# Second attention: signs of the fifth count used as a mask, copies and keeps regrouped, failing rows mended after the first keeps

## The chip, the cores and the metric

The kernel runs on one NeuronCore of a Trainium2 chip. The metric is the device time of one execution, in microseconds (us); less is better. The engines named below are TensorE (PE in the profile), VectorE (DVE), ScalarE (ACT), GpSimd (POOL) and SyncE (SP), each with its own queue of instructions. They meet only at semaphores. "Us" always means microseconds of the profiled execution unless a sentence says that it means the median of the runs.

## The reference, cut to what matters

A two-layer language-model tower on token ids of shape 2 x 1024, width 1024, 32 heads, 8 key/value heads, head width 32. The first layer is token mixing, causal attention and a top-2 mixture of experts; the second is an attention that keeps only 128 keys for each query, and a second mixture. The change lies in the second attention:

```python
qr = apply_rope(q, cos, sin)
kr = apply_rope(k, cos, sin)
draft = jnp.einsum('bhqd,bhkd->bhqk', qr, kr)
causal_future = qi[:, None] < ki[None, :]
draft = draft + jnp.where(causal_future, neg, jnp.asarray(0.0, dtype))
num_remain = max(min(Sq, MIN_REMAIN), Sq - int(Sq * MASK_OUT))      # 128
_, draft_indices = jax.lax.top_k(draft, num_remain)
mask = jnp.full((B, H, Sq, Sq), neg, dtype)
mask = mask.at[b_idx, h_idx, s_idx, draft_indices].set(0.0)
mask = jnp.where(causal_future[None, None, :, :], neg, mask)
scores = jnp.einsum('bhqd,bhkd->bhqk', qr, kr) / np.sqrt(HD).astype(np.float32) + mask
attn = jax.nn.softmax(scores, axis=-1)
out = jnp.einsum('bhqk,bhkd->bhqd', attn, v)
```

So each of the 2 x 32 x 1024 rows of scores needs its 128th largest value among its allowed keys; everything under it gets weight zero.

## The kernel before, in words

The program runs stage after stage: token mixing, projection, first attention, mixture, projection, second attention (`kept_attention`), mixture. All that changes is in `kept_attention` and in the constants that it reads.

**Tiles.** Heads go in pairs; there are 32 pairs. A pair has 16 tiles: for each of its two heads `m`, eight strips `i` of 128 queries, each (i+1)*128 keys wide (`TILES`). Strips with i = 0 have at most 128 keys and need no selection; the other 14 are `RANKED`, widths 256, 384, ... 1024 for each head. `x` holds the scores of a pair, `prob` their exponentials, both with two buffers.

**Slots.** The stage is a software pipeline in slots. In slot s four pairs are in hand: pair s+1 is scored (TensorE makes `ps_s`, VectorE moves it to `x`, `fetch`), pair s is searched (`count` on ScalarE, `narrow` on VectorE), pair s-1 is ranked and kept (VectorE: `rank_some`, `choose`, `exact_where_needed`, `keep`), and pair s-2 is multiplied with the values (TensorE transposes `prob` into `ps_t`, ScalarE copies it to `probT` in `evac`, TensorE multiplies by `v`, VectorE scales in `normalise`). Two slots make one turn of a hardware loop; four slots stand ahead of it and some behind.

**The search.** Each row has a threshold `t`. `start` sets it from mean and deviation of a sample of the row. Then five times (`PASSES`): ScalarE runs 14 activations Sign(t - x) with a sum (`count`, L1013), so the sum tells how many keys lie above t; VectorE waits for the last of them (`signs_done`) and moves t by a secant step on all 14 tiles at once (`narrow`, L1103 to L1134), where the count is more than 3.6 from the aim of 124.5; ScalarE waits for that (`t_ready`) ahead of its next pass. So a slot has five passes on ScalarE and five steps on VectorE, and each waits for the other.

**Ranking.** In the following slot VectorE makes, for each of the 14 tiles, three instructions (`rank_steps`): a compare with a sum that counts the keys at or over the sixth t and leaves a 0/1 mask `above` (L1145), a multiply-add that pushes those keys to -1e30 in `below` (L1147), and the eight largest of the rest (MAX8, L1150). If the count lies in 121..128, the 128th key is t itself or one of the eight. `choose` picks it for all rows; rows where that fails raise a flag, which is carried across partitions to one register. `exact_where_needed` loads that register and branches: with no failing row it jumps over a long body, else it runs `select_exactly` for the failing tiles, 16 rounds of MAX8 and MATCH_REPLACE over the whole tile.

**What else stands in the parts.** VectorE's work of a slot is written by hand in five parts, one ahead of each `narrow`: `RANKS` says which tiles are ranked in which part (parts 0 to 2), `KEEPS` which tiles are kept and fetched (parts 2 to 4), two keeps and two fetches in turn (`keep_and_fetch`, L1231 and L1241). `normalise` (L1262) stands in part 2, `invert` and `start` in part 4. ScalarE's copies `evac` (L983) are spread over its passes 0 and 1 by the table `after`, its exponentials over the ends of passes 2 and 3 (`EXPS`, L1025). `keep` (L1231) is one instruction a tile: (x >= limit) * prob with its sum.

The order of the work of a part, as the code has it:

```python
RANKS = [[*range(0, TT - 2), TT - 1], [TT - 2, *range(TT + 1, NS)], [TT], (), ()]
KEEPS = [(), (), range(0, 4), range(4, 14), range(14, 2 * TT)]
...
EVAC_PASSES = 2
...
EXPS = {2: range(0, TT + 3), 3: range(TT + 3, 2 * TT)}
```

## Time and profile before

| | us |
|---|---|
| median of 3 runs | 5799.51 |
| the runs | 5797.98 to 5799.66 |
| the profiled execution's own time | 5802.05 |
| its span (first to last instruction) | 5800.2 |
| mean granted TensorE clock over the span | 0.847 of full speed |
| busy: PE / DVE / ACT | 3975.3 / 3821.2 / 3315.8 |

In the page's 40 slices the second attention is the long even stretch from slice 18 to slice 37, where DVE and ACT both stand at 8 tenths and PE at 4 to 5:

```profile
PE   6997888888899989814555545555455554554599
...
DVE  1663666666233346458888888888888888888443
ACT  1113666666100011168888888888888888888200
...
PEclk7998999999999999956777777777777777777799
```

A busy engine is one that executes; where it waits for a semaphore or for its sequencer, it is idle, and the profile names what ended the wait. "issue" means that nothing the profile shows was waited for.

### The profile page before, as it was taken

Reading aid. Unit: us, or ns where it says so; the run is one execution under the profiler, and the core shown is the slowest. Engines: PE = TensorE matmul, PEld = TensorE weight load, DVE = VectorE, ACT = ScalarE, POOL = GpSimd, SP = SyncE. Lnnn points to the kernel's source line nnn. Section 1 sums busy time; section 2 is a strip of 40 time slices with the busy share of each in tenths; the row PEclk is TensorE's granted clock in tenths of the full one; section 3 lists DMA queues with packets and bytes.
Section 4 is the critical chain, followed back from the end, with each engine's and each line's share of the span. In section 5 each row is a group of like instructions: output and inputs, shape, how many; then the busy total and the mean of one; then the engine's idle time right before and its main releaser. Section 6 shows DMA issues by size and latency. Waiting matters only on the chain. (4 is left out here: it accounts for less than half of the span.)

```text
span 5800.2 us, 80523 instructions
## 1 busy us (share of the span) xinstructions
PE 3975.3 (69%) x23480; PEld 2373.9 (41%) x23480; DVE 3821.2 (66%) x10794; ACT 3315.8 (57%) x7698; POOL 289.1 (5%) x213
## 2 busy tenths in 40 slices
PE   6997888888899989814555545555455554554599
PEld 2444555555444444402333323333233332333354
DVE  1663666666233346458888888888888888888443
ACT  1113666666100011168888888888888888888200
POOL 1331000000000023300000000000000000000000
PEclk7998999999999999956777777777777777777799
DMA  3223222212311132310011010110101100010222
GB/s 122 68 68 70 61 56 48 69 47 50 113 44 43 43 101 68 72 30 21 4 24 23 21 23 4 23 23 21 22 5 23 23 21 17 10 23 5 69 66 80
DMA packets 277680, 250.19 MB, mean 43 GB/s; under 512 B 169968, under 2 KB 210048, under 8 KB 277248
## 3 DMA queue, kind: packets, MB, share of 16 engines
q1 hardware_dynamic: 276704, 245.60, 16.2%
q14 instruction: 313, 2.56, 0.2%
q8 instruction: 119, 1.95, 0.1%
q0 software_dynamic: 544, 0.07, 0.0%
HBM read 168.03 MB, written 77.59 MB: 42 GB/s over the span
## 5 line engine op out<-in xcount | busy, mean ns | idle before, releaser
L1013 ACT ACTIVATE a_sign<-a_x,a_state 128x256 fp8e4<-128x256 f32 (+6 forms) x2240 | 1833.7, 820 | 393.6 <-DVE a_state L1134 254.0
L922 PE MATMUL a_ps_s<-a_k,a_q 128*128 128x512 bf16 (+3 forms) x1536 | 479.5, 454 | 749.6 <-DVE a_x L1241 709.4
L950 PE MATMUL a_ps_o<-a_probT,a_v 128*32 128x128 f32 x4608 | 649.2, 289 | 461.8 <-ACT a_probT L983 457.1
L950 PEld LDWEIGHTS a_ps_o<-a_probT,a_v 128*32 128x32 f32 x4608 | 483.6, 115 | 597.3 <-ACT a_probT L983 548.9
L322 PE MATMUL p_ps_qkv<-p_w,p_hT 128*128 128x512 f32 x1536 | 676.6, 597 | 3.3 <-ACT p_hT L360 2.3
L701 ACT ACTIVATE a_prob<-a_ps_s,a_shift 128x640 f32<-128x640 f32 (+7 forms) x512 | 379.9, 742 | 349.0 <-DVE a_shift L743 304.0
L922 PEld LDWEIGHTS a_ps_s<-a_k,a_q 128*128 128x128 bf16 x1536 | 153.8, 123 | 986.6 <-DVE a_x L1241 809.6
L641 PE MATMUL a_ps_t<-a_ident,a_prob 128*128 128x128 f32 x2304 | 369.3, 286 | 164.8 <-ACT a_prob L701 100.9
L743 DVE TENSOR_REDUCE a_shift<-a_ps_s 128x1 f32<-128x640 f32 (+7 forms) x512 | 384.3, 753 | 111.2 <-PE a_ps_s L626 105.2
L322 PEld LDWEIGHTS p_ps_qkv<-p_w,p_hT 128*128 128x128 f32 x1536 | 289.1, 191 | 348.0 <-issue 344.9
L1145 DVE TENSOR_SCALAR_CACHE_REDUCE a_above<-a_x,a_state 128x256 bf16<-128x256 f32 (+3 forms) x448 | 391.8, 875 | 47.3 <-issue 38.2
L1013 ACT ACTIVATION_READ_ACCUMULATOR a_sign<-a_x,a_state 128x1 f32 x2240 | 422.8, 189 | 0.0
L1241 DVE TENSOR_SCALAR_CACHE_REDUCE a_x<-a_ps_s 128x128 f32<-128x128 f32 (+7 forms) x512 | 368.6, 756 | 65.2 <-issue 35.5
L933 PE MATMUL a_ps_t<-a_ident,a_prob 128*128 128x128 f32 x2304 | 409.8, 314 | 0.0
L983 ACT COPY a_probT<-a_ps_t 128x512 f32<-128x512 f32 (+3 forms) x768 | 349.9, 471 | 79.6 <-PE a_ps_t L933 78.9
L1150 DVE MAX8 a_nine<-a_below 128x8 f32<-128x256 f32 (+3 forms) x448 | 371.1, 828 | 33.0
L1231 DVE SCALAR_TENSOR_TENSOR a_prob<-a_x,a_limit,a_prob 128x256 f32<-128x256 f32 (+6 forms) x448 | 380.5, 881 | 10.5 <-issue 3.7
L753 DVE COPY a_probT<-a_ps_t 128x384 f32<-128x384 f32 (+3 forms) x384 | 222.0, 578 | 248.7 <-PE a_ps_t L641 245.2
L1147 DVE SCALAR_TENSOR_TENSOR a_below<-a_above,a_x 128x256 f32<-128x256 bf16 (+3 forms) x448 | 363.3, 811 | 7.2
L641 PEld LDWEIGHTS a_ps_t<-a_ident,a_prob 128*128 128x128 f32 x2304 | 252.3, 142 | 269.1 <-ACT a_prob L701 98.3
L623 PE MATMUL a_ps_s<-a_k,a_q 128*128 128x512 bf16 (+3 forms) x1536 | 339.9, 331 | 23.4 <-DMA a_v<-v 23.4
L1025 ACT ACTIVATE a_prob<-a_x,a_shift 128x256 f32<-128x256 f32 (+6 forms) x448 | 331.2, 813 | 0.0
(200 smaller groups left out, 5292.3 us busy)
## 6 DMA issues: line engine op xcount, KB each, us to landing
a_q<-qk SPq DMA_DIRECT2D x256, 256.0 KB, 4.9
qk<-p_qkT SPq DMA_DIRECT2D x32, 960.0 KB, 6.2
p_h<-h SPq DMA_DIRECT2D x32, 512.0 KB, 7.0
a_k<-qk SPq DMA_DIRECT2D x256, 64.0 KB, 5.1
m_o<-o SPq DMA_DIRECT2D x32, 512.0 KB, 5.4
m_h<-h SPq DMA_DIRECT2D x32, 512.0 KB, 5.5
p_w<-in_wqkv SPq DMA_DIRECT2D x16, 768.0 KB, 12.5
h<-tok_h SPq DMA_DIRECT2D x16, 512.0 KB, 2.6
```

The costliest lines, as they stand in the source:

```text
L322: m = nc.tensor.matmul(ps_qkv[:, n * BANK:(n + 1) * BANK], hT[:, par, k * P:(k + 1) * P], w[:, k, n * BANK:(n + 1) * BANK], start=(k == 0) ...
L641: mm = nc.tensor.transpose(ps_t[:, n % 2, c * P:(c + 1) * P], prob[:, s % 2, (a + c) * P:(a + c + 1) * P], ident[:, :])
L701: nc.scalar.activation(prob[:, s % 2, 0:w], ps_s[:, s % 2, 0:w], ACT.Exp, bias=shift[:, s % 4:s % 4 + 1], accum_out=total[:, u % 2, j:j + ...
L743: nc.vector.tensor_reduce(shift[:, c:c + 1], ps_s[:, s % 2, 0:(i + 1) * P], AX_X, ALU.max, negate=True).then_inc(shift_ready, 1)
L922: nc.tensor.matmul(ps_s[:, n % 2, a:a + w], q[:, y, head, i * P:(i + 1) * P], k[:, y, a:a + w], start=(y == 0), stop=False, skip_group_che ...
L933: mm = nc.tensor.transpose(ps_t[:, (n + 1) % 3, c:c + P], prob[:, par, at:at + P], ident[:, :])
L950: mm = nc.tensor.matmul(ps_o[strip:strip + DH, c:c + P], v[:, b * DH:(b + 1) * DH], probT[:, n % 2, b * P:(b + 1) * P], start=(b == 0), st ...
L1013: ins = nc.scalar.activation(sign[:, off(i):off(i) + w], x[:, par, at:at + w], ACT.Sign, scale=-1.0, saturate=False, bias=state[:, par, 0, ...
L1145: lambda: nc.vector.tensor_scalar(above[:, r, 0:w], x[:, y, at:at + w], tl, None, ALU.is_ge, ALU.add, accum_out=exact[:, n:n + 1]),
L1150: lambda: nc.vector.max(nine[:, n, 1:9], below[:, r, 0:w]),
L1231: nc.vector.scalar_tensor_tensor(out=prob[:, y, at:at + w], in0=x[:, y, at:at + w], scalar=limit[:, r:r + 1], in1=prob[:, y, at:at + w], o ...
L1241: nc.vector.tensor_scalar(x[:, y, at:at + w], ps_s[:, n % 2, 0:w], 1.0, None, ALU.mult, ALU.max, accum_out=top[:, y, n:n + 1]).then_inc(x_ ...
```

## The change

What it does, part by part.

1. **No count on VectorE, and no fifth `narrow`.** ScalarE's fifth pass writes its signs to a buffer of their own, `last` (fp8, all 14 tiles). In the next slot VectorE makes `below` as min(last * 2^116, x): where the sign is -1 (key over t) that is very low, else it is x. The sum of this instruction goes to `over`, and serves only to find keys equal to t. The rank comes from the signs' sum. So ranking is two instructions a tile instead of three, with the threshold of the fourth step instead of the fifth.
2. **The secant.** The brackets begin at a fixed distance of t (`REACH`, `BEND`) instead of at the row's maximum and at mean - 2.5 deviations; misses stand in the bracket instead of sums, ahead of the last step they are multiplied by `FADE`. Two clamps in the first `narrow` and five small copies in `start` go.
3. **Failing rows.** A row fails also if a key equals t. Failing rows get the limit `ALL_KEPT`, so their first `keep` keeps everything; then a code of the failing tiles is loaded to a register; where it isn't zero, `select_exactly` runs for the failing tiles, and tiles kept already are kept once more. The register is loaded, and the branch stands, behind seven keeps instead of ahead of all.
4. **Order.** Ranking stands wholly in parts 0 and 1, seven tiles each. Keeps: 7, 5, 2 tiles in parts 2, 3, 4. Fetches stand behind the keeps of their part in one row: 4, 8, 4 tiles. `normalise` comes behind the fetches of part 2. Exponentials: 6, 5, 5 tiles behind passes 2, 3, 4. The copies `evac` get a pause of 40 in the table between pass 0 and pass 1 and behind pass 1.
5. ScalarE waits for the last transpose of pair s-2 (`turn_done`) ahead of its exponentials, not for `normalise`. One more constant is loaded (`bits`).

```diff
-MASKED = -1e30
+MASKED = -1e18
+REACH, BEND = 600.0, 0.6
+CLOSE = 7.2
+FADE = 0.9
+WIDE = 2.0 ** 116
+ALL_KEPT = -1e17
...
-                    EVAC_PASSES = 2
-                    counted = [sum(2 + i for _, i in (RANKED * EVAC_PASSES)[:k]) for k in range(EVAC_PASSES * NS + 1)]
+                    EVAC_PASSES, BETWEEN = 2, 40
+                    counted = [sum(2 + i for _, i in (RANKED * EVAC_PASSES)[:k]) + BETWEEN * (k // NS)
+                               for k in range(EVAC_PASSES * NS + 1)]
...
-                            ins = nc.scalar.activation(sign[:, off(i):off(i) + w], x[:, par, at:at + w], ACT.Sign, scale=-1.0, saturate=False,
-                                                       bias=state[:, par, 0, n:n + 1], accum_out=state[:, par, 2, n:n + 1])
+                            to = last[:, at:at + w] if p == PASSES - 1 else sign[:, off(i):off(i) + w]
+                            ins = nc.scalar.activation(to, x[:, par, at:at + w], ACT.Sign, scale=-1.0, saturate=False,
+                                                       bias=state[:, par, 0, n:n + 1], accum_out=state[:, par, 3, n:n + 1])
...
-                    EXPS = {2: range(0, TT + 3), 3: range(TT + 3, 2 * TT)}
+                    EXPS = {2: range(0, 6), 3: range(6, 11), 4: range(11, 2 * TT)}
...
-                            lambda: nc.vector.tensor_scalar(above[:, r, 0:w], x[:, y, at:at + w], tl, None, ALU.is_ge,
-                                                            ALU.add, accum_out=exact[:, n:n + 1]),
-                            lambda: nc.vector.scalar_tensor_tensor(out=below[:, r, 0:w], in0=above[:, r, 0:w],
-                                                                   scalar=MASKED, in1=x[:, y, at:at + w], op0=ALU.mult,
-                                                                   op1=ALU.add),
+                            lambda: nc.vector.scalar_tensor_tensor(out=below[:, r, 0:w], in0=last[:, at:at + w],
+                                                                   scalar=WIDE, in1=x[:, y, at:at + w], op0=ALU.mult,
+                                                                   op1=ALU.min, accum_out=over[:, n:n + 1]),
...
                     def exact_where_needed():
 
-                        with dve.If_ne(raised(any_flag), 0):
-
-                            wait_alone(dve, exp_done, (s - 1) * (2 * TT) + 2 * TT, const_in, 64)
+                        dve.reg_load(which, failing[:, :])
+                        with dve.If_ne(which, 0):
+
+                            for k in (64, 32, 16, 8, 4, 2, 1):
+                                nc.vector.tensor_tensor(codes[:, 0:k], codes[:, 0:k], codes[:, k:2 * k], ALU.bitwise_or)
+                                dve.drain()
+                            dve.reg_load(which, codes[:, 0:1])
                             for n in range(NS):
-                                with dve.If_ne(raised(flag[:, n:n + 1]), 0):
+                                dve.reg_alu(this, which, 1 << n, ALU.bitwise_and)
+                                with dve.If_ne(this, 0):
                                     select_exactly(n)
+                                    if n in KEEPS[2]:
+                                        keep(n)
...
-                    RANKS = [[*range(0, TT - 2), TT - 1], [TT - 2, *range(TT + 1, NS)], [TT], (), ()]
-                    KEEPS = [(), (), range(0, 4), range(4, 14), range(14, 2 * TT)]
+                    RANKS = [range(0, TT - 1), range(TT - 1, NS), (), (), ()]
+                    KEEPS = [(), (), range(0, TT - 1), range(TT - 1, NS - 2), range(NS - 2, NS)]
+                    FETCHES = [(), (), range(0, 4), range(4, 12), range(12, 2 * TT)]
 
                     def part(p):
 
                         if st["keep"]:
+                            if p == 0:
+                                wait_alone(dve, signs_done, s * PASSES, const_in, 80)
                             rank_some(RANKS[p])
                             if p == 2:
                                 choose()
+                                dve.wait_ge(exp_done, (s - 1) * (2 * TT) + 2 * TT)
+                            for r in KEEPS[p]:
+                                keep(r).then_inc(prob_ready, 1)
+                            if p == 2:
                                 exact_where_needed()
+                            dve.drain()
+                        if st["score"]:
+                            for n in FETCHES[p]:
+                                fetch(n)
                         if p == 2 and st["value"]:
                             normalise()
-                        keep_and_fetch(KEEPS[p])
...
-                        if st["search"]:
+                        if st["search"] and p < PASSES - 1:
                             narrow(p)
```

In ScalarE's row of a steady slot, the end of pass 0 and the beginning of pass 1. L983 (L988 in the change) is the copy `evac`, L1013 (L1020) the Sign of one tile; the line L215 (L220) is where pass 1 waits for `t_ready`. Before:

```order
L1013 ACTIVATE a_sign,a_state<-a_x,a_state 128x896
L982 REGISTER_ALU
L983 COPY a_probT<-a_ps_t 128x512
L1013 ACTIVATE a_sign,a_state<-a_x,a_state 128x1024
L982 REGISTER_ALU
L983 COPY a_probT<-a_ps_t 128x512
L215 ISA
L1013 ACTIVATE a_sign,a_state<-a_x,a_state 128x256
```

And now:

```order
L1020 ACTIVATE a_sign,a_state<-a_x,a_state 128x1024
L987 REGISTER_ALU
L988 COPY a_probT<-a_ps_t 128x512
L987 REGISTER_ALU
L988 COPY a_probT<-a_ps_t 128x384
L987 REGISTER_ALU
L988 COPY a_probT<-a_ps_t 128x512
L987 REGISTER_ALU
L988 COPY a_probT<-a_ps_t 128x512
L220 ISA
L1020 ACTIVATE a_sign,a_state<-a_x,a_state 128x256
```

One copy stood between the last Sign and the wait; four stand there now, and fewer among the Signs.

In VectorE's row, the end of `choose` and what follows, up to the branch (TENSOR_LOAD is the load of the register, L1218 the `keep`):

```order
L1189 CAST a_codes<-a_codeT 1x32 x4
L1191 TENSOR_REDUCE a_failing<-a_codes 1x1
L1218 SCALAR_TENSOR_TENSOR a_prob,a_total<-a_x,a_limit,a_prob 128x256
L1218 SCALAR_TENSOR_TENSOR a_prob,a_total<-a_x,a_limit,a_prob 128x384
L1218 SCALAR_TENSOR_TENSOR a_prob,a_total<-a_x,a_limit,a_prob 128x512
L1218 SCALAR_TENSOR_TENSOR a_prob,a_total<-a_x,a_limit,a_prob 128x640
L1218 SCALAR_TENSOR_TENSOR a_prob,a_total<-a_x,a_limit,a_prob 128x768
L1218 SCALAR_TENSOR_TENSOR a_prob,a_total<-a_x,a_limit,a_prob 128x896
L1218 SCALAR_TENSOR_TENSOR a_prob,a_total<-a_x,a_limit,a_prob 128x1024
L1250 TENSOR_LOAD a_failing
L1251 COMPARE_AND_BRANCH
```

Seven keeps now stand between the reduction that gives the flag and the load of the flag; before, the load and the branch followed the reduction at once, and no keep stood ahead of them.

## Rows read from the trace of the kernel before

**Rows 1.** The page, busy time (us), share of the span, instructions, of three engines.

```profile
PE 3975.3 (69%) x23480; PEld 2373.9 (41%) x23480; DVE 3821.2 (66%) x10794; ACT 3315.8 (57%) x7698; POOL 289.1 (5%) x213
```

**Rows 2.** Line L1097, first threshold of each pair: count, first and last start.

```profile
L1097 DVE TENSOR_TENSOR a_state<-a_tmp,a_bracket x32: 174/175/176, 2497.9 to 5297.3; 128x14 f32<-128x14 f32 x32
```

**Rows 3.** One slot: length; busy PE, PEld, DVE, ACT, POOL; PEclk, DMA.

```profile
3474.20:3565.30 91.10, 48.20 (x284) 31.14 (x284) 77.31 (x247) 78.39 (x183) 0.00 (x0) 0.74 0.02 7
```

**Rows 4.** Waits from 2620 to 5290 us: who waited for whom, us, times, longest.

```profile
ACT a_sign L1013 <- DVE a_state L1134: 227.0, 87, 4.8
...
ACT a_sign L1013 <- DVE a_state L1097: 77.6, 29, 2.9
DVE a_o L1262 <- issue: 113.3, 29, 4.4
...
ACT a_probT L983 <- PE a_ps_t L933: 45.7, 69, 1.0
...
DVE a_side L1103 <- ACT a_sign L1013: 12.6, 17, 1.2
```

**Rows 5.** DVE in order of time: branch, last step, loop's end, clamps.

```profile
3525.59 0.69 DVE L1262 TENSOR_TENSOR a_o<-a_ps_o,a_invT 128x512 f32<-128x512 f32 x1 [4.31 <-issue]
...
3565.21 0.19 DVE L1103 TENSOR_TENSOR a_side<-a_state 128x28 int32<-128x28 f32 x1
...
3570.49 0.48 DVE L1145 TENSOR_SCALAR_CACHE_REDUCE a_above<-a_x,a_state 128x256 bf16<-128x256 f32 x1 [3.04 <-issue]
...
3586.70 0.17 DVE L1118 TENSOR_TENSOR a_new<-a_new,a_bracket 128x14 f32<-128x14 f32 x1
3586.95 0.17 DVE L1120 TENSOR_TENSOR a_new<-a_new,a_bracket 128x14 f32<-128x14 f32 x1
...
3590.66 0.08 DVE L1145 DVE_READ_ACCUMULATOR a_above<-a_x,a_state 128x1 f32 x1
3590.82 1.23 DVE L1150 MAX8 a_nine<-a_below 128x8 f32<-128x1024 f32 x1
3591.96 0.67 DVE L1147 SCALAR_TENSOR_TENSOR a_below<-a_above,a_x 128x512 f32<-128x512 bf16 x1
```

**Rows 6.** Groups from 2500 to 5420 us: count, busy us, mean ns, idle.

```profile
L1145 DVE TENSOR_SCALAR_CACHE_REDUCE a_above<-a_x,a_state 128x256 bf16<-128x256 f32 (+3 forms) x448 | 391.8, 875 | 47.3 <-issue 38.2
...
L1231 DVE SCALAR_TENSOR_TENSOR a_prob<-a_x,a_limit,a_prob 128x256 f32<-128x256 f32 x434 | 368.6, 881 | 9.8 <-issue 3.7
L1147 DVE SCALAR_TENSOR_TENSOR a_below<-a_above,a_x 128x256 f32<-128x256 bf16 (+3 forms) x448 | 363.3, 811 | 7.2
L1241 DVE TENSOR_SCALAR_CACHE_REDUCE a_x<-a_ps_s 128x128 f32<-128x128 f32 x496 | 356.9, 756 | 49.3 <-issue 35.5 <-PE a_ps_s L925 9.8
...
L1145 DVE DVE_READ_ACCUMULATOR a_above<-a_x,a_state 128x1 f32 x448 | 37.2, 83 | 0.0
```

**Rows 7.** PE in order of time: two score tiles, values, transposes.

```profile
3536.65 1.91 PE L922 MATMUL a_ps_s<-a_k,a_q 128*128 128x512 bf16 x4
3538.35 0.31 PE L925 MATMUL a_ps_s<-a_bias_b,a_ident_b 128*128 128x128 bf16 x1
...
3548.68 1.04 PE L922 MATMUL a_ps_s<-a_k,a_q 128*128 128x512 bf16 x4
...
3576.76 1.50 PE L950 MATMUL a_ps_o<-a_probT,a_v 128*32 128x128 f32 x12
3578.19 1.09 PE L933 MATMUL a_ps_t<-a_ident,a_prob 128*128 128x128 f32 x8
```

**Rows 8.** First attention, 600 to 1440 us: all waits ahead of L743.

```profile
DVE a_shift L743 <- PE a_ps_s L626: 80.3, 104, 1.2
```

**Rows 9.** ACT in order of time: first Sign of pass 2, its exponentials.

```profile
3514.89 0.51 ACT L1013 ACTIVATE a_sign<-a_x,a_state 128x256 fp8e4<-128x256 f32 x1 [4.36 <-DVE a_state L1134]
...
3526.44 0.39 ACT L1028 ACTIVATE a_prob<-a_x,a_shift 128x128 f32<-128x128 f32 x1
...
3526.82 5.13 ACT L1025 ACTIVATE a_prob<-a_x,a_shift 128x256 f32<-128x256 f32 x7
```

177 lines of the change are left out of this document (77 added, 100 removed).

## The prediction

> **What bounds the kernel now.** I began with the page's busy shares: no engine is above 69% [rows 1], so the bound changes with the stage, and the stage has to be read by itself. The first threshold of each pair is set 32 times between 2497.9 and 5297.3 us [rows 2], so a slot lasts (5297.3 - 2497.9) / 31 = 90.3 us, and whatever the change does comes times 31, with a little at the end. In one slot of 91.1 us ScalarE is busy for 78.4, VectorE for 77.3, TensorE for 48.2 [rows 3]. The table of waits says who holds whom [rows 4]: ScalarE's passes wait for VectorE 227.0 us for a step of the search and 77.6 for a pair's first threshold, and for TensorE 45.7. VectorE waits for ScalarE 12.6 us in the same stretch. So **VectorE's chain sets the slot**. ScalarE waits 227.0 + 77.6 + 45.7 = 350.3 of 2670 us, 13.1%: 11.8 of a slot of 90.3, and works 78.5. VectorE's own idle time is not a wait for others: 113.3 us in 29 times ahead of `normalise` (3.9 each) and 38.2 us [rows 6] ahead of the first ranking of a loop turn, both put down to "issue". The first is the load of the flag with the jump over the body of `exact_where_needed`, 4.31 us in one slot; the second is the loop's jump back, 3.04 us there [rows 5].
>
> **The change on VectorE**, per slot, minus is less:
> - The counting compare goes: (391.8 + 37.2) / 32 = -13.4 us [rows 6].
> - Its sum moves to the instruction that makes `below`. Without a sum that takes 811 ns in the mean, the same shape with a sum 881 [rows 6], and a read of the accumulator takes 83 ns with 70 more behind it for the drain [rows 5, 6]. 14 x (0.07 + 0.15) = +3.1. The first operand is fp8 now and was bf16; `below` takes 1.1 us for 1024 columns either way if the type costs nothing; no row shows fp8 as an operand here. Bounds: 0, as fp32 beside bf16 runs at one element a clock already, and +1 us.
> - The fifth step goes: it begins at 3565.21 and the idle time behind it at 3570.49 - 3.04 = 3567.45 [rows 5], -2.2. Two clamps at 0.25 from one start to the next [rows 5], and five copies and a drain in `start`, some 0.1 to 0.25 each, 0.8: -1.3. `choose` has as many instructions as before, within 0.3.
> - Fetches stand in a row now, so TensorE must score as fast as VectorE copies. A 1024-wide score tile takes 1.91 + 0.31 with overlap = 2.0 us in one place and 1.2 in another [rows 7]; a slot has 72 blocks of 128, nine such tiles: 18 or 11 us. VectorE's fetches take 356.9 / 31 = 11.5 [rows 6]. So between 0 and 6.5 us of new waits; two tiles stand scored ahead of each part, and I take +4.5.
> - The flag's load and jump: 3.9 in the mean [rows 4] stood with nothing queued; now seven keeps (half of 368.6 / 31 = 5.9 us [rows 6], plus reads) are queued ahead. If the sequencer works the load and jump off while the engine still works at the keeps, 0.5 is left; if the load waits until the engine is empty, all of it. Ends: -3.9 and 0. I take -3.4, since in the first attention, where the engines also jump back in a loop, VectorE's only waits ahead of its reductions are for TensorE, 1.2 us at most [rows 8], and there no drain stands ahead of the jump.
>
> The Trainium skill says on this, in "Advanced Engine Details and Errata", Sequencer Loop, that engine instructions are pushed to a queue and control instructions run on the sequencer, and in Engine Queue Depths that VectorE's queue holds 8; by that four keeps with their reads, some 4 us, would be left to cover the jump. No row here shows it.
>
> Sum: -12.7, so VectorE would need 77.6 a slot; but now **ScalarE is the bound**, at 78.5 of work. To that come its own waits. Behind pass 0 and behind pass 1 four copies stand together where one stood. TensorE needs 1.50 + 1.09 us and more for a wide tile's values and transposes, which is two copies [rows 7], so four need some 5.5 us against 1.9 of copying, less two chunks transposed ahead: 2 us twice, instead of the 1.5 that TensorE costs ScalarE now (45.7 / 29.6 slots [rows 4]): 4.3 in all. The two steps of the search behind passes 0 and 1 (1.4 and 2.2 us) hide beneath these copies. Handovers: five waits at some 0.3, 1.5 us. Slot: 78.5 + 4.3 + 1.5 = 84.3, less by 6.0.
>
> The tight places are parts 2 and 4. Part 2 on VectorE: `choose` 4.6, seven keeps 6.5, jump 0.5, four fetches with waits 3.1, `normalise` 0.7, step 2.2: 17.6. ScalarE covers it by pass 2, 11.6 (from 3514.89 to 3526.44), six exponentials, 3.6 out of the 5.1 for seven [rows 9], and the 2.3 by which its copies are late: 17.5. So they tie. Part 4: two keeps 2.3, fetches 5.8, `invert` 1.0, `start` 7.8, 16.9, against pass 4 and five exponentials, 15.9, with part 3 some 1 us ahead: a tie too. Other edits (the wait for `turn_done`, met long before; the constant `bits`; the fifth pass's other buffer) I cost at nothing: none lies behind a late releaser. Behind the last start the ranking of the last pair is shorter by 10 us and nothing covers it.
>
> So without failing rows: 31 x 6.0 + 10 = **-196 us**.
>
> **Mending** is the other large term. Before there was a sixth threshold and a count that took keys equal to t; the trace of before has no instruction of `select_exactly`. Following the changed search in float32 on the reference's inputs, of the 32 x 14 x 128 = 57,344 ranked rows one misses 121..128: pair 7, head 0, widest strip, with counts 182, 99, 116, 120, 129, and it does so also with the scores disturbed by 1 in 10,000. Besides, a key equals t in 0.9 rows by expectation (density of keys at t times the spacing of floats), which can't be said for certain from outside. So one mend has 4 chances in 10, two have 4, three or more 2. A mend stops VectorE at a tie, so all of it counts. Its 16 rounds for 1024 columns: MAX8 1.15 net [rows 5], MATCH_REPLACE unseen, taken as the same as both pass once over the row (from half to twice of it), two drains 0.15, a jump back 0.2: 42 us; around it some 10 (copy, compare, predicated copy, keep, the codes, 14 branches): 52. For a middle width 43. The loop's jump is bounded by nothing and by the 3.04 of the slot loop, +49 a mend; that loop's body has hundreds of instructions and this one has four, so I take near nothing.
>
> The Trainium skill speaks for that: "Runtime: NRT & Kernel Launch", Instruction fetch mechanics, has a taken branch pay for a fetch only where its target is outside a window of two pages. "Advanced Engine Details and Errata", Control Flow Timing, gives 108 ns for a compare and branch; by it the 16 rounds would hold 1.7 us of jumps.
>
> **Forecast**: two mends, 52 + 43 = +95. The profiled execution took 5802.05, 2.5 above the median of the runs: 5802 - 196 + 95 = 5701 for the profiled one, 5699 against the median; I say 5700. With one mend 5656, with three 5742.
>
> **Rivals.**
> 1. *The jump stays in sight.* If the load waits for an empty engine, part 2 takes 21.4 on VectorE instead of 17.6 and ScalarE waits for it: 3.8 x 31 = 118 us given back. 5700 + 118 = 5818 with two mends, **slower** by 0.3%; with one 5775. It turns the sign from 101 / 31 = 3.3 us of exposed jump a slot. For it: the drain ahead of the load in both kernels, and the 4.31 us of idle time [rows 5], which comes behind small instructions that could have covered some of it. Against: the keeps ahead of it now.
> 2. *Mending is dear.* With 3.0 a jump back each mend costs 49 more: two mends make 5798, no change; three 5889, slower. It decides from 196 us of mends. Against it: the tiny body.
> 3. *VectorE stays the bound through the scores.* If TensorE is at the slow row's 2.0 a tile all along, parts 3 and 4 are late by 2.5 us: 78 us given back, 5778. For it: the mean granted clock of 0.74 of full speed in the slot [rows 3], so half of it at the lower of the two levels, 1.2 GHz. Against: eight tiles in a row keep it busier than two.
>
> **How the numbers follow.** A difference of 0.2% (12 us) is about what can be told from none. Chances: forecast 0.50 (one to three mends: 5656 to 5742), rival 1 0.25, rival 2 0.13, rival 3 0.12. Faster by over 0.2%: 0.48 of the forecast's, 0.10 of rival 1 (one mend), 0.06 of rival 2 (one mend), 0.08 of rival 3: 0.72. Within: 0.09. Slower: rival 1 with two or more mends 0.13, and 0.06 from the others: 0.19. Range: 5645 to 5825, from one mend with part of the waits of TensorE missing to rival 1 with two mends; the forecast's own is 5645 to 5755.
>
> **What would show it.** In the profile after: starts of pairs some 84 us apart instead of 90.3 (88 for rival 1); VectorE's idle time behind the seventh keep of part 2 under 1 us (about 4 for rival 1); ScalarE's wait for pass 3 near nothing, its waits for TensorE grown from 1.5 to about 4 a slot; MATCH_REPLACE 16 times for each mend, 32 in all, and one place or two where the starts lie 45 us further apart. The forecast is wrong if passes 0 and 1 still wait for the steps, if more than three mends are there, or if the stretch between two starts stays over 87 us.

## The result, and the profile after

The changed kernel takes **5652.41 us** in the median (5645.80 to 5654.25, four runs) against 5799.59 before: ratio 0.9746, 95% interval 0.9731 to 0.9761. The forecast was 5700, in a range of 5645 to 5825. The profiled execution took 5654.25 and has a span of 5652.4; all that follows is read from it.

The page's busy shares of the kernel after, line L1097 (count, duration in ns, first and last start), and two slots, each from one first threshold to the next (length, then busy us and instructions by engine, PEclk, DMA, GB/s):

```profile
PE 3967.2 (70%) x23480; PEld 2387.8 (42%) x23480; DVE 3478.4 (62%) x9793; ACT 3308.1 (59%) x7698; POOL 288.7 (5%) x213
```

```profile
L1097 DVE TENSOR_TENSOR a_state<-a_tmp,a_mv x32: 173/174/176, 2496.8 to 5173.6; 128x14 f32<-128x14 f32 x32
```

```profile
3609.50:3691.80 82.30, 45.84 (x284) 30.41 (x284) 63.87 (x210) 78.25 (x183) 0.00 (x0) 0.79 0.08 19
3691.80:3775.20 83.40, 49.35 (x284) 32.22 (x284) 63.88 (x210) 78.26 (x183) 0.00 (x0) 0.73 0.11 22
```

The 31 slots last 2799.4 - 2676.8 = 122.6 us less than before [rows 2], and what follows the last start another 24 (5652.4 - 5173.6 = 478.8, before 5800.2 - 5297.3 = 502.9). ScalarE works as long in a slot as it did (78.3; 78.4 before), VectorE 63.9 instead of 77.3 [rows 3]. The 31 stretches are not alike. Three are long, 138.6, 121.1 and 115.9 us, the first two are short (69.4, 77.2), and the plain ones last **82.7 us** in the mean (those of 75 to 100 us; before 91.0). In the long ones ScalarE stands still while VectorE mends, which here means that it runs `select_exactly` for a failing tile. ScalarE in order of time (start, length; in brackets the idle time and who ended it), and VectorE's MATCH_REPLACE8, one in each round of a mend:

```profile
3248.15 0.51 ACT L1020 ACTIVATE a_sign<-a_x,a_state 128x256 fp8e4<-128x256 f32 x1 [56.46 <-DVE a_state L1134]
...
4030.53 0.51 ACT L1020 ACTIVATE a_sign<-a_x,a_state 128x256 fp8e4<-128x256 f32 x1 [37.94 <-DVE a_state L1134]
...
4312.25 0.51 ACT L1020 ACTIVATE a_sign<-a_x,a_state 128x256 fp8e4<-128x256 f32 x1 [33.73 <-DVE a_state L1134]
```

```profile
L1204 DVE MATCH_REPLACE8 a_below<-a_best,a_below x48: 542/675/1210, 3192.4 to 4302.7; 128x1024 f32<-128x1024 f32 x16, 128x512 f32<-128x512 f32 x16, 128x384 f32<-128x384 f32 x16
```

48 replacements are three mends of 16 rounds: 1024, 512 and 384 columns wide. They lengthen their slots by 55.9, 38.4 and 33.2 us over a plain one, 127.5 together. Without them the 31 slots would have lost 250 us, 8.1 each.

The waits of the kernel after, 2500 to 5130 us (us in total, times, longest), which answer to [rows 4]:

```profile
DVE a_state L1108 <- ACT a_sign L1020: 235.9, 69, 11.7
DVE a_x L1228 <- PE a_ps_s L930: 156.7, 250, 1.0
ACT a_sign L1020 <- DVE a_state L1134: 140.0, 18, 56.5
ACT a_probT L988 <- PE a_ps_t L938: 96.5, 89, 3.0
...
ACT a_sign L1020 <- DVE a_state L1097: 21.8, 29, 1.4
```

The table has turned round: VectorE waits for ScalarE's signs, 235.9 us where it was 12.6. ScalarE's 227.0 us for the steps of the search are 140.0, of which 128.1 are the three rows above, so 11.9 in plain slots; for the pairs' first thresholds it waits 21.8 instead of 77.6. Its waits for TensorE doubled, 45.7 to 96.5.

The jump over the mending, on VectorE in a plain slot, first the engine's rows, then its sequencer's (duration ns, start):

```profile
3731.87 0.48 DVE L1218 SCALAR_TENSOR_TENSOR a_prob<-a_x,a_limit,a_prob 128x256 f32<-128x256 f32 x1 [0.19 <-issue]
...
3736.31 1.28 DVE L1218 SCALAR_TENSOR_TENSOR a_prob<-a_x,a_limit,a_prob 128x1024 f32<-128x1024 f32 x1
3737.52 0.08 DVE L1218 DVE_READ_ACCUMULATOR a_prob<-a_x,a_limit,a_prob 128x1 f32 x1
3737.87 0.29 DVE L1228 TENSOR_SCALAR_CACHE_REDUCE a_x<-a_ps_s 128x128 f32<-128x128 f32 x1 [0.27 <-issue]
```

```profile
L1250 DVEq TENSOR_LOAD <-a_failing x1: 317/317/317, 3732.4 to 3732.4; - x1
```

```profile
L1251 DVEq COMPARE_BRANCH  x1: 72/72/72, 3732.8 to 3732.8; - x1
```

```profile
L1265 DVEq DRAIN  x1: 2102/2102/2102, 3735.6 to 3735.6; - x1
```

VectorE's sequencer (whose rows hold its register loads, branches and drains) loads at 3732.4 and is behind the jump at 3735.6, while the engine works at its keeps until 3737.6. The drain there then waits 2.1 us for the engine. Of the 4.31 us ahead of `normalise` [rows 5], 0.27 are left.

Where in a slot each of the two engines waits: VectorE's steps of the search behind passes 1 and 2 in that slot, and ScalarE's pass 3:

```profile
3724.69 0.17 DVE L1108 TENSOR_TENSOR a_state<-a_state,a_table 128x14 f32<-128x14 f32 x1 [4.64 <-ACT a_sign L1020]
...
3741.38 0.17 DVE L1108 TENSOR_TENSOR a_state<-a_state,a_table 128x14 f32<-128x14 f32 x1
```

```profile
3743.55 0.51 ACT L1020 ACTIVATE a_sign<-a_x,a_state 128x256 fp8e4<-128x256 f32 x1 [0.40 <-DVE a_state L1134]
```

In the mean of the plain slots VectorE waits 1.95 us ahead of the step behind pass 0, 4.8 behind pass 1, and 0.0 and 0.1 behind passes 2 and 3. ScalarE waits for it 0.2 ahead of pass 3 and nothing ahead of passes 1, 2 and 4.

### The profile page after: what moved, and what is told of

It is laid out like the page before. It is cut to its first block and busy times, and to the rows that moved or that the text cites. A ratio compares the mean times of both kernels' runs of the same rounds, so it can differ in the third digit from the quotient of the medians.

```text
span 5652.4 us, 79291 instructions
## 1 busy us (share of the span) xinstructions
PE 3967.2 (70%) x23480; PEld 2387.8 (42%) x23480; DVE 3478.4 (62%) x9793; ACT 3308.1 (59%) x7698; POOL 288.7 (5%) x213
## 3 DMA queue, kind: packets, MB, share of 16 engines
q8 instruction: 119, 1.95, 0.1%
## 5 line engine op out<-in xcount | busy, mean ns | idle before, releaser
L1020 ACT ACTIVATE a_sign<-a_x,a_state 128x256 fp8e4<-128x256 f32 (+6 forms) x1792 | 1466.9, 821 | 219.0 <-DVE a_state L1134 140.0
L938 PE MATMUL a_ps_t<-a_ident,a_prob 128*128 128x128 f32 x2304 | 417.5, 314 | 22.1 <-ACT a_probT L988 21.8
L988 ACT COPY a_probT<-a_ps_t 128x512 f32<-128x512 f32 (+3 forms) x768 | 344.5, 472 | 132.7 <-PE a_ps_t L938 132.7
L1142 DVE SCALAR_TENSOR_TENSOR a_below<-a_last,a_x 128x256 f32<-128x256 fp8e4 (+6 forms) x448 | 362.7, 810 | 48.2 <-issue 36.2
L1145 DVE MAX8 a_nine<-a_below 128x8 f32<-128x256 f32 (+6 forms) x448 | 371.2, 829 | 33.4 <-issue 0.4
L1218 DVE SCALAR_TENSOR_TENSOR a_prob<-a_x,a_limit,a_prob 128x512 f32<-128x512 f32 (+6 forms) x450 | 370.8, 883 | 11.6 <-issue 5.2
L646 PEld LDWEIGHTS a_ps_t<-a_ident,a_prob 128*128 128x128 f32 x2304 | 252.5, 142 | 268.9 <-ACT a_prob L706 98.4
L1020 ACT ACTIVATE a_last<-a_x,a_state 128x256 fp8e4<-128x256 f32 (+6 forms) x448 | 364.2, 814 | 2.2
L938 PEld LDWEIGHTS a_ps_t<-a_ident,a_prob 128*128 128x128 f32 x2304 | 283.9, 157 | 139.2 <-issue 88.3
L1020 ACT ACTIVATION_READ_ACCUMULATOR a_sign<-a_x,a_state 128x1 f32 x1792 | 340.8, 190 | 0.0
## 6 DMA issues: line engine op xcount, KB each, us to landing
p_w<-in_wqkv SPq DMA_DIRECT2D x16, 768.0 KB, 11.9
```

The lines of the kernel that those rows point to most:

```text
L646: mm = nc.tensor.transpose(ps_t[:, n % 2, c * P:(c + 1) * P], prob[:, s % 2, (a + c) * P:(a + c + 1) * P], ident[:, :])
L938: mm = nc.tensor.transpose(ps_t[:, (n + 1) % 3, c:c + P], prob[:, par, at:at + P], ident[:, :])
L1020: ins = nc.scalar.activation(to, x[:, par, at:at + w], ACT.Sign, scale=-1.0, saturate=False, bias=state[:, par, 0, n:n + 1], accum_out=sta ...
L1142: lambda: nc.vector.scalar_tensor_tensor(out=below[:, r, 0:w], in0=last[:, at:at + w], scalar=WIDE, in1=x[:, y, at:at + w], op0=ALU.mult, ...
L1145: lambda: nc.vector.max(nine[:, n, 1:9], below[:, r, 0:w]),
L1218: return nc.vector.scalar_tensor_tensor(out=prob[:, y, at:at + w], in0=x[:, y, at:at + w], scalar=limit[:, r:r + 1], in1=prob[:, y, at:at ...
```

## The experiments

The theory: VectorE's chain was the bound; the counting compare and the hidden jump took it below ScalarE's, which bounds the slot now with its 78.3 us of work, its waits for TensorE and the handovers; three mends stand on VectorE's chain and take back 127 us. The rivals to be told from it: the compare or the jump never mattered; ScalarE's order of work doesn't matter; a mend can be covered. "Plain" is the mean distance of two starts, of those of 75 to 100 us, the second slot (77.2) included; "long" is what the stretches of over 100 us are over it. Each interval compares a run with executions of the kernel before that were taken beside it; their medians lie between 5795.2 and 5799.6. No run takes the fifth step of the search or the new brackets by themselves.

| run | median us | to before (95% interval) | plain | long |
|---|---|---|---|---|
| before | 5799.6 | | 91.0 | |
| after | 5652.4 | 0.9731 to 0.9761 | 82.7 | 55.9, 38.4, 33.2 |
| 1 jump exposed | 5771.8 | 0.9936 to 0.9969 | 87.0 | 52.8, 35.3, 29.5 |
| 2 no mend | 5520.1 | 0.9504 to 0.9536 | 82.7 | |
| 3 before, no jump | 5717.0 | 0.9843 to 0.9876 | 88.3 | |
| 4 count back | 5895.8 | 1.0152 to 1.0186 | 90.0 | 59.5, 36.1, 38.4 |
| 5 no pause | 5713.3 | 0.9834 to 0.9867 | 84.7 | 55.5, 38.1, 33.8 |
| 6 exponentials early | 5726.0 | 0.9859 to 0.9892 | 85.1 | 54.3, 35.1, 30.8 |
| 7 in turns | 5636.8 | 0.9704 to 0.9737 | 82.1 | 56.0, 38.3, 33.3 |
| 8 mend written out | 5682.6 | 0.9787 to 0.9819 | 82.6 | 66.2, 51.2, 41.8 |
| 9 no test for equal keys | 5649.6 | 0.9732 to 0.9764 | 82.7 | 56.8, 37.5, 33.1 |
| 10 mend behind step | 5638.9 | 0.9709 to 0.9741 | 81.9 | 59.9, 39.2, 35.2 |
| 11 turns, pause 30 | 5620.8 | 0.9680 to 0.9713 | 81.5 | 56.4, 38.3, 33.6 |
| 12 same, equal key ranked | 5561.9 | 0.9576 to 0.9608 | 82.0 | 56.4 |

### 1. The jump in sight

```diff
+                        dve.drain()
                         dve.reg_load(which, failing[:, :])
```

> The changed kernel with one drain of VectorE's queue ahead of the load of the failing flag, so that the load and the compare-and-branch come only once the seven keeps have ended, as they did before the change. If the jump's hiding is worth something, the 3.1 us that VectorE's sequencer took from load to branch end stand on VectorE's chain again and the mends start as late as in the changed kernel: +3 to +4 us per plain slot, starts about 86 apart instead of 82.8, +95 to +125 us in all, about 5760. If ScalarE alone bounds the slot now and VectorE has 7.6 us a slot to spare in its waits for the signs, the exposed jump falls into that slack for the most part: under +1 us a slot, under +30 us in all, about 5665.

119 us slower than the changed kernel. The drain makes the load wait until the keeps are done. VectorE's sequencer, its next fetch, and ScalarE's pass 3 in that slot:

```profile
L1251 DVEq TENSOR_LOAD <-a_failing x1: 315/315/315, 3702.6 to 3702.6; - x1
```

```profile
3708.32 0.29 DVE L1228 TENSOR_SCALAR_CACHE_REDUCE a_x<-a_ps_s 128x128 f32<-128x128 f32 x1 [5.85 <-issue]
```

```profile
3713.99 0.51 ACT L1020 ACTIVATE a_sign<-a_x,a_state 128x256 fp8e4<-128x256 f32 x1 [5.53 <-DVE a_state L1134]
```

VectorE's idle time at this place is 3.5 to 3.8 us in 15 plain slots and 5.6 to 6.1 in 12; in the changed kernel it is 0.27 or less in all of these. ScalarE takes it over almost whole at pass 3, ahead of which it waits 4.5 us in the mean of the plain slots instead of 0.2. So the slack that VectorE has by the table of waits is no help: it lies ahead of the steps behind passes 0 and 1 (1.95 and 4.8 us, and as much in this run), not in part 2. Rival 1 of the prediction, made on purpose, costs what it was priced at (118).

### 2. No mend

```diff
-                            if p == 2:
-                                exact_where_needed()
```

> The changed kernel without its call of the mending: failing rows stay whole (the rows that fail keep every probability, so the output differs there). It prices the three mends and the jump together. If the three long slots are all that the mends cost and the jump is hidden, the plain slots stay at 82.8 us and the three of 138.6, 121.1 and 115.9 fall to 82.8: -127 us, about 5525. If the hidden jump still costs some of the plain slots (the fetches behind it come up to 1 us late each slot), the plain slots fall too, to 81.8 or so: -155 us, about 5495. If a slot after a mend had been short because the others ran ahead, part of the 127 was paid back already: -110 us, about 5542.

132 us faster, and the plain slots are the same to 0.1 us (2493.7 to 5043.0 for the 31 slots, 127.5 less than with mends). So load and jump cost nothing more where they are hidden, and the three long slots are the mends' whole price.

```profile
L1097 DVE TENSOR_TENSOR a_state<-a_tmp,a_mv x32: 173/174/175, 2493.7 to 5043.0; 128x14 f32<-128x14 f32 x32
```

### 3. The kernel before without the jump

```diff
-                        dve.reg_load(any_raised, any_flag[0:1, :])
-                        return any_raised
...
-                        with dve.If_ne(raised(any_flag), 0):
...
-                        dve.drain()
+                        raised(any_flag)
+                        wait_alone(dve, exp_done, (s - 1) * (2 * TT) + 2 * TT, const_in, 64)
```

> The kernel before, with its flag of raised rows still reduced and copied, but neither loaded nor tested, and without the select behind it that never ran: this leaves out the mending. It prices the jump by itself where VectorE was the bound. If the 3.2 us from load to branch end plus the register load stood fully on the chain: -3.9 us a slot, starts 86.4 apart instead of 90.3, -120 us in all, about 5680. If the fetches then wait for TensorE's scores instead (which end at their own pace), only part of it is won: -2 us a slot, about 5740. If the jump never bounded anything: 5800.

82 us, 2.7 a slot: between the two. Its waits, 2620 to 5210 us:

```profile
ACT a_sign L1013 <- DVE a_state L1134: 196.7, 58, 4.9
...
ACT a_sign L1013 <- DVE a_state L1097: 33.0, 29, 1.2
...
DVE a_o L1260 <- issue: 15.6, 29, 0.6
```

Ahead of `normalise` 113.3 - 15.6 = 98 us of idle time went, and ScalarE waits (227.0 + 77.6) - (196.7 + 33.0) = 75 us less for VectorE. The rival of TensorE's scores isn't borne out, VectorE waits 6.2 us for them. So of 3.4 us of idle time in a plain slot 2.7 came back. The rest went mostly into 0.3 us more of waits for signs and 0.2 of busy time on VectorE.

### 4. The count back on VectorE

```diff
+                            lambda: nc.vector.tensor_scalar(below[:, r, 0:w], x[:, y, at:at + w], tl, None, ALU.is_ge,
+                                                            ALU.add, accum_out=exact[:, n:n + 1]),
...
```

> The changed kernel with the counting compare of the 14 rows put back on VectorE, its count not used (one more drain a tile than before the change, some 0.07 us each, as the compare shares a buffer with the clamp). It adds 13.4 us and the 1 us of drains to VectorE in each slot. If the slack of VectorE's waits for signs (7.6 us a slot) absorbs what it can and VectorE bounds the slot again: +14.4 - 7.6 = +6.8 us a slot, +210 us in all, about 5860, starts 89.5 apart. If the compare was never on the path (ScalarE's passes set the slot before, too): under +1 us a slot, about 5670. If it stands whole on the path, since it sits where the signs of the next slot's first passes are waited for: +14.4 a slot, +445 us, about 6100.

243 us slower, and 1.7% slower than the kernel before. Two slots, each from start to start:

```profile
3605.80:3698.40 92.60, 50.41 (x282) 33.27 (x284) 76.16 (x238) 78.59 (x183) 0.00 (x0) 0.74 0.10 21
3698.40:3786.90 88.50, 50.16 (x282) 33.45 (x284) 76.16 (x237) 78.57 (x183) 0.00 (x0) 0.73 0.07 17
```

VectorE's work is 12.3 us more, a plain slot 7.3: the rest filled the slack ahead of the first two steps, where VectorE now waits 0.2 us each instead of 1.95 and 4.8. With the count on VectorE the change loses, since all its other edits together win some 1 to 2 us a slot (90.0 with 1 us of added drains, against 91.0) and the three mends cost 134 here. That is little for a jump that is worth 2.7 (run 3) and a step of 2.2 less; against them stand the fetches in a row, for which VectorE waits 144.2 us here from 2500 to 5130, about 5 a slot. The gain hangs on the count, and by run 1 on the hidden jump as well: without either of them most of it is gone.

### 5 and 6. ScalarE's order of work

```diff
-                    EVAC_PASSES, BETWEEN = 2, 40
+                    EVAC_PASSES, BETWEEN = 2, 0
```

> The changed kernel with ScalarE's probability copies spread over passes 0 and 1 as before (no allowance of 40 between the passes, so two to four copies stand behind the last count of pass 0 no more). Now the copies run inside the two passes and nothing lies between them while VectorE narrows. If those four copies fill ScalarE's wait for the thresholds of pass 1, as the change has them placed, the wait comes back for about 1.9 us a slot: +58 us, about 5712, starts 84.7 apart. If ScalarE's wait for the transposes (3.1 us a slot) is what the later copies cause, the return takes that away and both balance: 5640 to 5665. If TensorE, which gets its transposed tiles sooner, had been the bound of the fetches: under 5640.

```diff
-                    EXPS = {2: range(0, 6), 3: range(6, 11), 4: range(11, 2 * TT)}
+                    EXPS = {2: range(0, TT + 3), 3: range(TT + 3, 2 * TT)}
```

> The changed kernel with the exponentials as before the change: eleven behind pass 2, five behind pass 3, none behind pass 4. If part 2 of VectorE's work (the seven keeps, which run while ScalarE does its exponentials behind pass 2) is tied with ScalarE's part at 17.6 against 17.5 us and the later parts are what ScalarE needs filled, ScalarE waits at passes 3 and 4 again and VectorE waits longer for pass 3: +2.8 us a slot, +85 us, about 5738, starts 85.6 apart. If ScalarE's work alone, wherever it stands, bounds the slot (78.5 us of it are the same): under +0.5 us a slot, 5650 to 5668.

+61 and +74 us, 2.0 and 2.4 a slot, with the same work on every engine. Waits, 2500 to 5130 us, first without the pause, then with the exponentials early:

```profile
ACT a_sign L1020 <- DVE a_state L1134: 249.8, 89, 57.7
...
ACT a_probT L988 <- PE a_ps_t L938: 36.2, 50, 1.0
```

```profile
ACT a_sign L1020 <- DVE a_state L1134: 125.9, 7, 53.2
ACT a_sign L1020 <- DVE a_state L1097: 102.0, 28, 4.3
```

The pause trades waits for TensorE (96.5 against 36.2) for more than they are worth in waits for steps (140.0 against 249.8). The exponentials had another effect than I expected: not passes 3 and 4 wait, but pass 0 of the next pair (102.0 against 21.8), for nothing stands behind pass 4 to cover part 4 with `start`.

### 7. Keeps and fetches in turn

```diff
-                            for r in KEEPS[p]:
-                                keep(r).then_inc(prob_ready, 1)
...
+                        while keeps or fetches:
+                            if keeps:
+                                keep(keeps.pop(0)).then_inc(prob_ready, 1)
+                                dve.drain()
+                            for n in fetches[:2]:
+                                if st["score"]:
+                                    fetch(n)
+                            fetches = fetches[2:]
```

> The changed kernel with the keeps and the fetches of parts 3 and 4 issued in turn (one keep, two fetches), so that a fetch comes no sooner than TensorE has its scores; in the changed kernel the fetches that follow one another wait for TensorE 5 us a slot in all. If ScalarE bounds the slot, VectorE only trades this wait for a longer one on the signs: 5640 to 5665, starts 82.5 to 82.8 apart, the 156.7 us of waits behind fetches under 80 and the 235.9 us for signs over 300. If the fetches' waits still bind through the start of the next search: -1 us a slot, about 5620. If the in-order keeps come later and hold up TensorE's transposes of the probabilities: slower, 5670 or more.

16 us faster than the changed kernel, 0.6 a slot. VectorE's wait for the scores fell from 156.7 to 66.0 us and that for signs rose from 235.9 to 297.2, as the theory has it; but something of it did count. That fits parts 2 to 4 being a tie of the two engines, where both wait 0.2 us or less in the changed kernel; which part gave the 0.6 isn't shown.

```profile
DVE a_state L1108 <- ACT a_sign L1020: 297.2, 94, 11.7
...
DVE a_x L1228 <- PE a_ps_s L930: 66.0, 151, 1.0
```

### 8. The mend written out

```diff
-                        with dve.Fori(0, KEEP // 8):
+                        for _ in range(KEEP // 8):
```

> The changed kernel with the sixteen rounds of a mend written out in place of a loop (two instructions a round for each of the fourteen tiles, skipped in nearly every slot). In the loop a round of 1024 takes 2.93 us, of which 0.34 is idle for the jump back. If that idle is all that the loop costs: -0.34 x 16 x 3 = -16 us, about 5636, plain slots unchanged at 82.8. If the longer code that the branch now jumps over (over 400 instructions more) must be fetched anew, the hidden jump of 2.8 us grows and shows: +1 us a slot or more, over 5680. If the written-out rounds themselves stall while their code is fetched, a mend is no shorter or longer than before: 5650 to 5700.

30 us slower. VectorE in the wide mend, in order of time:

```profile
3198.23 0.69 DVE L1199 COPY a_below<-a_x 128x1024 f32<-128x1024 f32 x1 [8.90 <-issue]
3199.00 1.23 DVE L1202 MAX8 a_best<-a_below 128x8 f32<-128x1024 f32 x1
3200.30 0.09 DVE L1204 MATCH_VALUE_LOAD a_below<-a_best,a_below 128x8 f32 x1
3200.38 1.21 DVE L1204 MATCH_REPLACE8 a_below<-a_best,a_below 128x1024 f32<-128x1024 f32 x1
3201.66 1.23 DVE L1202 MAX8 a_best<-a_below 128x8 f32<-128x1024 f32 x1
...
3253.18 0.29 DVE L1228 TENSOR_SCALAR_CACHE_REDUCE a_x<-a_ps_s 128x128 f32<-128x128 f32 x1 [7.76 <-issue]
```

and of the changed kernel, with the loop:

```profile
3190.19 0.69 DVE L1199 COPY a_below<-a_x 128x1024 f32<-128x1024 f32 x1 [2.53 <-issue]
3191.04 1.23 DVE L1202 MAX8 a_best<-a_below 128x8 f32<-128x1024 f32 x1 [0.15 <-issue]
...
3193.99 1.23 DVE L1202 MAX8 a_best<-a_below 128x8 f32<-128x1024 f32 x1 [0.36 <-issue]
...
3242.48 0.29 DVE L1228 TENSOR_SCALAR_CACHE_REDUCE a_x<-a_ps_s 128x128 f32<-128x128 f32 x1 [1.20 <-issue]
```

A round takes 3201.66 - 3199.00 = 2.66 us instead of 3193.99 - 3191.04 = 2.95, so the loop costs 0.3 a round. But the thirteen branches over tiles that don't fail now jump over longer bodies: 8.90 us ahead of the mend instead of 2.53, 7.76 behind it instead of 1.20. By the rows of its sequencer (L1259, from one of these branches to what follows) six of the thirteen take 2.0 to 2.5 us each (3190.7 to 3193.1, 3193.5 to 3195.5 and 3195.6 to 3198.1 ahead of the mend, three more behind it) and the other seven 0.2 to 0.5; in the changed kernel none takes over 0.6. What sets the six apart isn't shown. The time came out where the second expectation had it, over 5680, but not by its way: the plain slots are unchanged, and their one jump takes 2.8 to 3.1 us from branch to next instruction (2.8 to 3.2 in the changed kernel).

### 9 and 12. Which mends are these?

```diff
-                        nc.vector.scalar_tensor_tensor(out=fail[:, :], in0=equal[:, :], scalar=0.5 - 2 * AIM,
+                        nc.vector.scalar_tensor_tensor(out=fail[:, :], in0=equal[:, :], scalar=1e6,
```

> The changed kernel whose test for a key equal to the threshold has a bound that is never reached, with as many instructions (this leaves out that rows with such a key are made to fail). It tells which mends are misses of the search and which are equal keys. If the search misses once (pair 7, 1024 columns) and the other two mends are equal keys, one mend is left: 16 MATCH_REPLACE8, all of 1024 columns; the slots of 121.1 and 115.9 fall to 82.8, -71 us, about 5581. If all three are misses of the search, nothing changes: 5652 and 48 of them. If the wide one is an equal key too, none is left: -127 us, about 5525.

Nothing changed, 48 replacements as before. My reading of that outcome was wrong, not the theory: one key equal to t has a sign of 0, which makes the rank a half by itself, so the row fails without the test. Hence the last run, on the fastest version (11 below):

```diff
-                        nc.vector.tensor_scalar(rank[:, :], off_aim, 0.5, KEEP - AIM, ALU.mult, ALU.add)
+                        nc.vector.tensor_scalar(whole[:, :], off_aim, 0.5, KEEP - AIM - 0.25, ALU.mult, ALU.add)
...
+                        nc.vector.tensor_copy(rank[:, :], whole[:, :])
+                        dve.drain()
...
-                        nc.vector.scalar_tensor_tensor(out=fail[:, :], in0=equal[:, :], scalar=0.5 - 2 * AIM,
+                        nc.vector.scalar_tensor_tensor(out=fail[:, :], in0=equal[:, :], scalar=1.5 - 2 * AIM,
```

> The version in turns with the pause of 30 (5621), in which one key equal to the threshold no longer makes its row fail. The run without the test for equal keys could not tell the mends apart, since one equal key also makes the sum of signs odd and the rank a half, which matches no place and fails the row by itself. Here the rank is rounded down through an integer, and the test for equal keys fails a row only from two such keys on; for a threshold over zero the row is then picked by the same keys, for one under zero it keeps one key less (this leaves out the mending of such rows). Two small instructions and a drain are added to VectorE's part 2, some 0.2 us a slot. If the two narrower mends (512 and 384 columns) are equal keys and the wide one a miss of the search: 16 MATCH_REPLACE8 instead of 48, one long slot, -72 us and up to +7 for the rounding, 5549 to 5556. If all three are misses of the search (the rank outside 0 to 7): 48 still, 5621 to 5628. If the wide one is an equal key too: none left, about 5495.

```profile
L1206 DVE MATCH_REPLACE8 a_below<-a_best,a_below x16: 1208/1209/1211, 3190.9 to 3234.8; 128x1024 f32<-128x1024 f32 x16
```

One mend is left, the wide one at the same place; 5561.9, 59 us less than version 11. So the 512 and the 384 wide mends were single equal keys. The wide one isn't, and it stands where the search was forecast to miss. The mends gone are worth 71.9; the rounding costs 0.4 us in each plain slot instead of 0.2, 13 us in all.

### 10. The mend behind the step

```diff
                         with dve.If_ne(which, 0):
+                            if st["search"]:
+                                narrow(2)
+                                dve.drain()
...
+                        if st["search"] and p == 2 and st["keep"]:
+                            with dve.If_eq(again, 0):
+                                narrow(p)
...
```

> The version with keeps and fetches in turn (5637), in which a slot with a failing row does the third step of the search ahead of the mend instead of behind it (the step stands in the branch of the mend, and a second branch skips it behind the fetches), so that ScalarE has pass 3 and its exponentials to do while VectorE mends. If ScalarE's idle time in a mend (56 us in one) is what it costs, each mend costs less by the 17 us of that work: -50 us, about 5587. If a mend costs what VectorE's own chain from the mend to the next start takes, which is not shortened since VectorE waits for no signs there, the three long slots stay within 2 us of 138.1, 120.4 and 115.4: 5632 to 5637. If the second branch drains VectorE's queue or jumps in sight in each plain slot: +0.5 to +3 us a slot, 5650 to 5730.

5638.9 against 5636.8: nothing won. ScalarE does its pass 3 beside the mend and then waits as long for pass 4:

```profile
ACT a_last L1020 <- DVE a_state L1134: 128.8, 3, 56.5
```

The long slots are 1 to 4 us longer still. A mend costs what VectorE's chain from there to the next start takes, whatever ScalarE does meanwhile. The second branch, whose body runs in each plain slot, costs nothing that shows (81.9 against 82.1).

### 11. A pause of 30, in turns

```diff
-                    EVAC_PASSES, BETWEEN = 2, 40
+                    EVAC_PASSES, BETWEEN = 2, 30
```

> The version with keeps and fetches in turn, and the pause between ScalarE's passes 30 instead of 40, so that three copies stand behind pass 0 in a row instead of four, and four behind pass 1 instead of five. ScalarE waits 99.3 us for TensorE's transposes there, 3.2 a slot, as a row of copies outruns TensorE. If a shorter row lets it catch up: -0.5 to -1 us a slot, 5605 to 5625. If the copies taken out leave ScalarE waiting for the thresholds of passes 1 and 2 instead: no change or slower, 5635 to 5660.

5620.8: 16 us less than version 7, 0.5 a slot, and with all of the computation done it is the fastest: 31.6 us (0.6%) under the changed kernel, 3.0% under the one before.

```profile
ACT a_sign L1020 <- DVE a_state L1134: 170.9, 34, 57.3
...
ACT a_probT L988 <- PE a_ps_t L938: 40.9, 58, 1.2
```

Both sides of the trade are there: 58 us less of waits for TensorE, 35 more for steps (135.7 in version 7).

## Why the prediction was right, and where its terms were off

**The mechanism held.** VectorE's chain was the bound: without its jump the kernel before is 82 us faster (run 3), and with the count back the changed one is 243 us slower (run 4). ScalarE is the bound now, together with a tie in parts 2 to 4. VectorE's work fell by 77.3 - 63.9 = 13.4 us; its terms of work were -13.4 + 3.1 - 2.2 - 1.3 = -13.8. The fp8 operand costs nothing: the line that makes `below` takes 810 ns in the mean with its sum, 811 without one before, so even the 0.07 for the sum isn't there:

```profile
L1142 DVE SCALAR_TENSOR_TENSOR a_below<-a_last,a_x 128x256 f32<-128x256 fp8e4 (+6 forms) x448 | 362.7, 810 | 48.2 <-issue 36.2 <-ACT a_last L1020 8.9
```

- **Fetches in a row**: taken as 4.5 a slot between 0 and 6.5; measured are 156.7 / 31 = 5.1, of which 2.9 go with fetches in turn for a gain of 0.6. Rival 3 is out.
- **The jump**: -3.4 taken, 0.27 left. Forced into sight it costs 4.3 a slot and 119 in all (run 1). So rival 1 had the right price and the wrong premise. The Trainium skill, "Advanced Engine Details and Errata", Engine Queue Depths, gives VectorE a queue of 8. When the load ran, at 3732.4, six keeps and their reads were still running or to come, twelve instructions by the profile's rows; the page holds here only if a keep and its read count as one.
- **ScalarE's waits, the step that was mis-sized**: 4.3 + 1.5 = 5.8 a slot forecast, 4.2 measured. (Its two rows of copies at 2 us each make 4.0, not 4.3.) For TensorE 96.5 / 31 = 3.1, for the first thresholds 21.8 / 31 = 0.7, for steps 11.9 / 31 = 0.4. Where VectorE's threshold stands ready in time, ScalarE's pass starts without a wait (passes 1, 2 and 4 above), where I took 0.3 for each of five. Thus 82.7 instead of 84.3 in a plain slot, and over the 31 slots, the short first ones included, 250 us gained instead of 31 x 6.0 = 186: 64 more.
- **The end**: -24 us instead of -10. Behind the last start there is one more search with all the gains of a slot, which I had not counted; up to its fourth step 5236.44 - 5173.58 = 62.9 us now and 5368.15 - 5297.25 = 70.9 before. And from the last Sign of the last pair to its first keep it takes 5279.13 - 5249.98 = 29.2 us now and 5429.59 - 5382.55 = 47.0 before, 17.9 less where I had 10.

```profile
5236.44 0.17 DVE L1108 TENSOR_TENSOR a_state<-a_state,a_table 128x14 f32<-128x14 f32 x1 [9.35 <-ACT a_sign L1020]
```

```profile
5368.15 0.19 DVE L1103 TENSOR_TENSOR a_side<-a_state 128x28 int32<-128x28 f32 x1 [6.92 <-ACT a_sign L1013]
```

- **The mends**: the wide one was forecast in its place (pair 7) at 52 and took 55.9; a round is 2.95 instead of the 2.6 assumed. The ends are lighter than "a middle width, 43": 38.4 and 33.2. There were three where two were taken, so 127.5 instead of 95; three or more had 2 chances in 10 in the text. Two single equal keys against an expectation of 0.9 can be chance; nothing here tests the expectation.
- **Rival 2** is refuted: the jump back costs 0.3 us, not 3.0. The Trainium skill, "Advanced Engine Details and Errata", Control Flow Timing, has 108 ns for a compare and branch; here a turn of the loop costs some 290 ns over a written-out round (run 8).

Together: 5802 (the profiled time of before) - 250 + 127.5 - 24 = 5655.5, of the 5654.3 that the profiled execution after took. The forecast's 5701 was 47 too slow: 64 + 14 of gains that were too small, less 32 for the third mend. That the time lies in the range at all is luck: the third mend hid part of the error. With the two mends that the forecast reckoned with it would have been 5652.4 - 33.2 = 5619, under the range's lower end of 5645.

## What to carry to other kernels

A branch on data costs VectorE 3.5 to 6.1 us here if its queue is empty when the flag is loaded, and 0.3 or less if six microseconds of ready work are queued ahead; so put it behind such work, with no drain in between. When an engine's work is cut and the bound goes over to another one, count the waits inside each part and not their sum in the slot: VectorE had 7.6 us of slack a slot, and an exposed jump still came through almost whole (4.3 us), since the slack lay in other parts. Rare work on the chain, here the mends, is priced by its length alone: covering it with the other engine's work gave nothing (run 10), and making it rarer gave its full price (run 12).

## What the runs showed of the hardware that I had not expected

- The same jump costs 3.5 to 3.8 us in some plain slots and 5.6 to 6.1 in others (run 1); in one slot of the dearer kind the jump took from 3702.9 to 3705.7, and 2.6 more went by ahead of the next fetch. The jump itself takes 2.8 us in the cheap kind too (3615.3 to 3618.1), where the fetch follows after 0.3. In the hardware loop, whose turn holds two slots, the two kinds alternate, so the dearer one goes with one of the two copies of the slot's code. What happens in these 2.6 us was not tried.
- Written-out code can be dearer though its rounds are quicker: run 8 paid 6.4 and 6.6 us more around the mend, in steps of 2.0 to 2.5 us at six of thirteen branches over longer bodies. The Trainium skill, "Runtime: NRT & Kernel Launch", Instruction fetch mechanics, says that a taken branch to code outside the window of two pages has to wait for its fetch. The rows agree in direction, and no run measured the window.
- A MATCH_REPLACE8 over 1024 columns takes 1.21 us with 0.09 for loading its eight values, as long as the MAX8 of 1.23.
